# Head projections of a ViT tower in split format: resonances written twice, weights stacked

## The reference, cut to what matters

```python
def holo_linear(x, basis, phase, amp):
    resonance = jnp.einsum('bli,hi->blh', x, basis)      # 32 harmonics
    w = amp * jnp.cos(phase)
    return jnp.einsum('blh,oh->blo', resonance, w)
q = split_heads(holo_linear(x, basis_q, phase_q, amp_q))
k = split_heads(holo_linear(x, basis_k, phase_k, amp_k))
v = split_heads(holo_linear(x, basis_v, phase_v, amp_v))
attn = jax.nn.softmax(jnp.einsum('bhqd,bhkd->bhqk', q, k) * scale, axis=-1)
```

## Time and profile before

| what | us |
|---|---|
| median of 3 runs | 2207.89 (2204.55 to 2208.34) |
| the profiled execution | 2204.59 |
| its span in the trace | 2202.8 |
| outside the span | 1.8 |
| stage_a with its set-up, about | 0 to 1130 |
| one step of stage_a in the middle | 33.54 (key projections at 560.07 and 593.61) |
| PE busy, of the span | 2081.1 |

### The profile page before, as it was taken

How to read it: one execution, slowest core, us unless ns; L and a number is a source line. 1 busy time by engine, 2 the same in 40 slices (tenths; PEclk the granted TensorE clock), 3 DMA queues, 4 the chain that set the end, 5 groups by cost and what they waited for, 6 DMA issues and landing times. The chain is left out here.

```text
span 2202.8 us, 42583 instructions
## 1 busy us (share of the span) xinstructions
PE 2081.1 (94%) x15678; PEld 1847.7 (84%) x15678; DVE 1436.8 (65%) x3061; ACT 991.9 (45%) x2044; POOL 684.3 (31%) x737
## 2 busy tenths in 40 slices
PE   5899999999999999999889999999999999999998
PEld 4677777787887877777758999989998888889998
DVE  7677777777777877777644444677754444445666
ACT  2155555455555555554553333322225555554332
POOL 4334334233243343342202111000013333333665
PEclk9999999999999999999999999999999999999999
DMA  2533433424334233344214343000013333334665
GB/s 76 84 66 64 85 62 77 81 54 89 70 65 85 66 73 82 62 80 71 50 39 155 120 135 130 27 23 30 30 44 99 106 104 104 106 103 121 183 182 157
DMA packets 125274, 189.25 MB, mean 86 GB/s; under 512 B 23153, under 2 KB 76418, under 8 KB 125074
## 3 DMA queue, kind: packets, MB, share of 16 engines
q1 hardware_dynamic: 101232, 134.65, 26.0%
q0 software_dynamic: 12736, 34.69, 5.6%
q10 hardware_dynamic: 11106, 17.19, 2.4%
HBM read 84.32 MB, written 49.58 MB: 61 GB/s over the span
## 5 line engine op out<-in xcount | busy, mean ns | idle before, releaser
L675 ACT ACTIVATE pT<-ps 128x514 f32<-128x514 f32 x512 | 304.9, 597 | 308.7 <-PE ps L485 304.0
L842 DVE TENSOR_REDUCE mx<-ps 128x2 f32<-128x512 f32 x512 | 340.7, 680 | 106.1 <-PE ps L468 106.0
L2001 POOL DMA_INDIRECT z<-zd,itab x136 | 128.3, 944 | 470.2 <-DVE itab L1914 253.5
L468 PE MATMUL ps<-km,q 112*128 112x256 f32 x1024 | 246.0, 327 | 16.3 <-DMA km<-klo 10.5
L485 PE MATMUL ps<-q,km 114*128 114x258 f32 x1024 | 228.7, 305 | 31.5 <-ACT pT L675 31.5
L485 PEld LDWEIGHTS ps<-q,km 114*128 114x128 f32 x1024 | 159.1, 189 | 81.0 <-ACT pT L675 54.3
L1291 PE MATMUL ps<-zhi,whi 128*128 128x256 f32 x1056 | 218.4, 289 | 2.5 <-issue 2.4
L468 PEld LDWEIGHTS ps<-km,q 112*128 112x128 f32 x1024 | 166.7, 191 | 58.3 <-issue 24.9
L1291 PE MATMUL ps<-zhi,wlo 128*128 128x256 f32 x1056 | 214.7, 285 | 0.0
L1291 PE MATMUL ps<-zlo,whi 128*128 128x256 f32 x1056 | 213.9, 284 | 0.0
L1319 ACT ACTIVATE sil<-ps 128x512 f32<-128x512 f32 x132 | 79.0, 598 | 264.6 <-PE ps L1291 264.6
(11 more groups left out here) (320 smaller groups left out, 4997.5 us busy)
## 6 DMA issues: line engine op xcount, KB each, us to landing
yd<-raws SPq DMA_DIRECT2D x136, 128.0 KB, 1.8
q<-qhi SPq DMA_DIRECT2D x128, 129.0 KB, 4.1
km<-khi SPq DMA_DIRECT2D x256, 64.5 KB, 3.2
xs<-in_x SPq DMA_DIRECT2D x64, 256.0 KB, 4.4
z<-hscr SPq DMA_DIRECT2D x46, 256.0 KB, 2.9
raws<-in_wu SPq DMA_DIRECT2D x12, 768.0 KB, 4.8
hscr<-h SPq DMA_DIRECT2D x34, 256.0 KB, 5.1
zd<-z SPq DMA_DIRECT2D x33, 256.0 KB, 2.0
```

What stands on the lines that cost most here:

```text
L468: last = pe.matmul(ps[:, i % 2, k * L:(k + 1) * L], q2[p % U][0:MAXROW, QAT[g], t * P:(t + 1) * P], km[p % 2][0:MAXROW, k, g, 0:L], start= ...
L675: act.activation(pT[:, 2 * g:2 * g + 2, t, :], ps[:, score_bank(b, n):score_bank(b, n) + 2, 0:N], ACT.Exp, scale=HD ** -0.5).then_inc(s_ok, 1)
L842: dve.tensor_reduce(mx[:, t, 2 * QAT[g]:2 * QAT[g] + 2], ps[:, i % 2, :].rearrange("p (k l) -> p k l", k=2), AX_X, ALU.max, negate=True).t ...
L2001: pool.indirect_dma_start(zg(i), None, zd_rows, bass.IndirectOffsetOnAxis(itab[:, i:i + 1], 0)).then_inc(zg_in[i % NG], 16)
```

## The change

`resonances` has 128 output rows in place of 96: the basis of the queries is laid down a second time behind q, k and v. ACT writes all 128 rows rounded to `rhi` (float32r). Then ACT copies the rounded rows of the keys (rows 32 to 63 of `rhi`) to rows 96 to 127 of a second tile `rlo`, and DVE (`res_low`) writes the remainder, PSUM minus `rhi`, to rows 0 to 95 of `rlo`. A weight tile `wst` holds for q and k the rounded weight in its own 32 rows and the weight's remainder in rows 96 to 127, and for v the rounded weight and its remainder in two slots. A projection of q or k is then two float32r matmuls for each half of the channels (one over 96 rows, one over 128), one of v is three for each half of the positions. `Wz` moves to a temporary area and serves only the class token; the class token's resonances go to `rcls`. `res_low` stands in DVE's list at n = 3 behind `mixer_ekv`. `heads_qk(j, 0)` waits for both writes of ACT and for DVE's.

```diff
-    basT = sb("basT", [P, FT, 3 * HARM])
+    basT = sb("basT", [P, FT, P])
-    Wz = sb("Wz", [3 * HARM, 3, D])
+    wst = sb("wst", [P, 4, D], F32R)
-    rT = sb("rT", [3 * HARM, NP])
+    rcls = sb("rcls", [3 * HARM, NP - L])
+    rhi = sb("rhi", [P, L], F32R)
+    rlo = sb("rlo", [P, L], F32R)
+    Wz = temp(3, D)[0:3 * HARM]
...
-                last = pe.matmul(ps[0:3 * HARM, 6, 0:L], basT[:, f, :], zT[:, f, 0:L], ...)
+                last = pe.matmul(ps[:, 6, 0:L], basT[:, f, :], zT[:, f, 0:L], ...)
...
         def heads_qk(j, n):
             if n == 0:
-                pe.wait_ge(r_ok, j + 1)
+                if j == 0:
+                    pe.wait_ge(w_ok, 2)
+                pe.wait_ge(r_ok, 2 * j + 2)
+                pe.wait_ge(rl_ok, j + 1)
             else:
                 pe.wait_ge(lo_ok, 2 * j + 1)
+            whole, part = ((rhi, rlo), (rlo, rhi))[n]
             for f in range(FT):
-                last = pe.matmul(ps[:, 6, f * L:(f + 1) * L], Wz[:, n, f * P:(f + 1) * P], rT[:, 0:L], start=True, stop=True)
+                pe.matmul(..., wst[0:3 * HARM, n, f * P:(f + 1) * P], part[0:3 * HARM, :], start=True, stop=False)
+                last = pe.matmul(..., wst[:, n, f * P:(f + 1) * P], whole[:], start=False, stop=True)
...
         def heads_v(m):
-                last = pe.matmul(..., rT[:, t * P:(t + 1) * P], Wz[:, 2, :], start=True, stop=True)
+                mm = ((rhi, 2), (rlo, 2), (rhi, 3))
+                for i, (x, n) in enumerate(mm):
+                    last = pe.matmul(..., x[0:3 * HARM, t * P:(t + 1) * P], wst[0:3 * HARM, n, :], ...)
...
                     if n == 3:
                         act.wait_ge(r_ps, b + 3)
-                        act.activation(rT[:, 0:L], ps[0:3 * HARM, 6, 0:L], ACT.Copy).then_inc(r_ok, 1)
+                        if later(b + 2):
+                            act.wait_ge(v_ps, b + 2)
+                        act.activation(rhi[:], ps[:, 6, 0:L], ACT.Copy).then_inc(r_ok, 1)
+                        act.wait_ge(r_ok, 2 * b + 5)
+                        act.activation(rlo[3 * HARM:P, :], rhi[HARM:2 * HARM, :], ACT.Copy).then_inc(r_ok, 1)
...
+        def res_low(j):
+            dve.wait_ge(r_ok, 2 * j + 1)
+            dve.tensor_tensor(rlo[0:3 * HARM, :], ps[0:3 * HARM, 6, 0:L], rhi[0:3 * HARM, :], ALU.subtract).then_inc(rl_ok, 1)
...
                 if has(b + 3) and n in (2, 3):
                     mixer_ekv(b + 3, n - 2)
+                if has(b + 2) and n == 3:
+                    res_low(b + 2)
...
         dve.memset(Wz[:], 0.0)
+        dve.memset(wst[:].bitcast(F32), 0.0)
...
+        dve.wait_ge(w_ok, 1)
+        for n in range(2):
+            rows = slice(n * HARM, (n + 1) * HARM)
+            dve.tensor_copy(wst[rows, n, :], Wz[rows, n, :])
+        rows = slice(2 * HARM, 3 * HARM)
+        chain(dve.tensor_copy(wst[rows, 2, :], W[rows, :]))
+        for n in range(2):
+            rows = slice(n * HARM, (n + 1) * HARM)
+            dve.tensor_tensor(wst[3 * HARM:P, n, :], Wz[rows, n, :], wst[rows, n, :], ALU.subtract)
+        rows = slice(2 * HARM, 3 * HARM)
+        dve.tensor_tensor(wst[rows, 3, :], W[rows, :], wst[rows, 2, :], ALU.subtract).then_inc(w_ok, 1)
```

More of the change, by code:

```diff
@@ L175, in stage_a @@
     clso = sb("clso", [P, G, B])
-    (c_load, c_set, d_step, half_ok, mask_ok, wb_ok, ew_ok, arg_ok, cos_ok, w_ok, clsvar_ok, clsrs_ok, clsz_ok, clsT_ps,
-     clsT_ok, clsr_ps, clsr_ok, clsqkv_ps, spread_ok, mix_in) = (
+    (c_load, c_set, d_step, half_ok, mask_ok, wb_ok, ew_ok, arg_ok, cos_ok, w_ok, clsvar_ok, clsrs_ok, clsz_ok, cls_ps,
+     clsT_ok, clsr_ok, spread_ok, mix_in) = (
         sem(x) for x in ("c_load", "c_set", "d_step", "half_ok", "mask_ok", "wb_ok", "ew_ok", "arg_ok", "cos_ok", "w_ok",
-                         "clsvar_ok", "clsrs_ok", "clsz_ok", "clsT_ps", "clsT_ok", "clsr_ps", "clsr_ok", "clsqkv_ps",
+                         "clsvar_ok", "clsrs_ok", "clsz_ok", "cls_ps", "clsT_ok", "clsr_ok",
                          "spread_ok", "mix_in"))
@@ L191, in stage_a @@
     wo_in, vb_ok, vb_in, roh_ok = sem("wo_in"), sem("vb_ok"), sem("vb_in"), sem("roh_ok")
+    rl_ok = sem("rl_ok")
     r_ps, r_ok, qk_ps, v_ps, v_ok, hi_ok, lo_ok = (
@@ L420, in resonances @@
             for f in range(FT):
-                last = pe.matmul(ps[0:3 * HARM, 6, 0:L], basT[:, f, :], zT[:, f, 0:L], start=(f == 0), stop=(f == FT - 1))
+                last = pe.matmul(ps[:, 6, 0:L], basT[:, f, :], zT[:, f, 0:L], start=(f == 0), stop=(f == FT - 1))
             last.then_inc(r_ps, 1)
@@ L426, in heads_qk @@
             if n == 0:
-                pe.wait_ge(r_ok, j + 1)
+                if j == 0:
+                    pe.wait_ge(w_ok, 2)
+                pe.wait_ge(r_ok, 2 * j + 2)
+                pe.wait_ge(rl_ok, j + 1)
             else:
                 pe.wait_ge(lo_ok, 2 * j + 1)
+            whole, part = ((rhi, rlo), (rlo, rhi))[n]
             for f in range(FT):
-                last = pe.matmul(ps[:, 6, f * L:(f + 1) * L], Wz[:, n, f * P:(f + 1) * P], rT[:, 0:L], start=True, stop=True)
+                pe.matmul(ps[:, 6, f * L:(f + 1) * L], wst[0:3 * HARM, n, f * P:(f + 1) * P], part[0:3 * HARM, :], start=True, stop=False)
+                last = pe.matmul(ps[:, 6, f * L:(f + 1) * L], wst[:, n, f * P:(f + 1) * P], whole[:], start=False, stop=True)
             last.then_inc(qk_ps, 1)
@@ L437, in heads_v @@
             for t in range(LT):
-                last = pe.matmul(ps[:, 6, t * D:(t + 1) * D], rT[:, t * P:(t + 1) * P], Wz[:, 2, :], start=True, stop=True)
+                mm = ((rhi, 2), (rlo, 2), (rhi, 3))
+                for i, (x, n) in enumerate(mm):
+                    last = pe.matmul(ps[:, 6, t * D:(t + 1) * D], x[0:3 * HARM, t * P:(t + 1) * P], wst[0:3 * HARM, n, :],
+                                     start=(i == 0), stop=(i == len(mm) - 1))
             last.then_inc(v_ps, 1)
@@ L608, in _ @@
             last = pe.matmul(ps[:, 6, f:f + 1], clsz[:, f * P:(f + 1) * P], one1[:], start=True, stop=True)
-        last.then_inc(clsT_ps, 1)
+        last.then_inc(cls_ps, 1)
         pe.wait_ge(clsT_ok, 1)
         for f in range(FT):
-            last = pe.matmul(ps[0:3 * HARM, 5, 16:17], basT[:, f, :], zT[:, f, CLS:N], start=(f == 0), stop=(f == FT - 1))
-        last.then_inc(clsr_ps, 1)
+            last = pe.matmul(ps[0:3 * HARM, 5, 16:17], basT[:, f, 0:3 * HARM], zT[:, f, CLS:N], start=(f == 0), stop=(f == FT - 1))
+        last.then_inc(cls_ps, 1)
         pe.wait_ge(clsr_ok, 2)
@@ L617, in _ @@
             for f in range(FT):
-                pe.matmul(ps[:, 4, n * FT + f:n * FT + f + 1], Wz[:, n, f * P:(f + 1) * P], rT[:, CLS:N], start=True,
+                pe.matmul(ps[:, 4, n * FT + f:n * FT + f + 1], Wz[:, n, f * P:(f + 1) * P], rcls[:, 0:1], start=True,
                           stop=True)
         pe.matmul(ps[0:NH, 7, 0:D], rbc[:], Wz[:, 2, :], start=True,
-                  stop=True).then_inc(clsqkv_ps, 1)
+                  stop=True).then_inc(cls_ps, 1)
         filler(5, 12)
@@ L757, in _ @@
         act.activation(tr[:], tn[:], ACT.Sin).then_inc(cos_ok, 1)
-        act.wait_ge(clsT_ps, 1)
+        act.wait_ge(cls_ps, 1)
         act.activation(zT[:, :, CLS:N], ps[:, 6, 0:FT].rearrange("p (f o) -> p f o", o=1), ACT.Copy).then_inc(clsT_ok, 1)
-        act.wait_ge(clsr_ps, 1)
-        act.activation(rT[:, CLS:NP], ps[0:3 * HARM, 5, 16:17].broadcast_to([3 * HARM, 2]), ACT.Copy).then_inc(clsr_ok, 1)
+        act.wait_ge(cls_ps, 2)
+        act.activation(rcls[:], ps[0:3 * HARM, 5, 16:17].broadcast_to([3 * HARM, 2]), ACT.Copy).then_inc(clsr_ok, 1)
         mixer_norm(0, 0)
@@ L990, in _ @@
         dve.wait_ge(clsr_ok, 1)
-        dve.tensor_copy(rbc[:], rT[:, CLS:N].broadcast_to([3 * HARM, NH])).then_inc(clsr_ok, 1)
+        dve.tensor_copy(rbc[:], rcls[:, 0:1].broadcast_to([3 * HARM, NH])).then_inc(clsr_ok, 1)
         attn_stats(0, 0)
-        dve.wait_ge(clsqkv_ps, 1)
+        dve.wait_ge(cls_ps, 3)
         chain(dve.tensor_copy(clsh[:], ps[:, 4, 0:2 * FT].rearrange("p (n f) -> p n f", n=2)))
@@ L2067, in layout @@
     o["lnb"] = f(np.tile(t["tok_ln_b"][None], (P, LT)))
-    o["basT"] = tiles(np.concatenate([t["attn_basis_" + n].T for n in "qkv"], axis=1))
+    o["basT"] = tiles(np.concatenate([t["attn_basis_" + n].T for n in "qkvq"], axis=1))
     o["basoT"] = tiles(np.tile(t["attn_basis_o"].T, (1, 3)))
```

## The result

The changed kernel takes 2230.39 us in the median (4 runs, 2224.74 to 2232.83), the kernel before 2208.11 beside it (4 runs, 2204.55 to 2209.77). The ratio is 1.0097, with a 95% interval from 1.0077 to 1.0118: 17 to 26 us slower. The profiled execution took 2224.74 with a span of 2222.9, which is 20.1 us more than before.

A forecast was written before the change was run, and what follows sets the result against it. PE was busiest, but DVE set the stretch to L398. 30 steps x 0.61 = 18.3 plus 1.3 set-up made 19.6 us: 2224.2 from the profiled execution, 2227.5 from the median, forecast 2226, range 2217 to 2236.

The forecast's parts named there:

- The wait and its cause: Queries' projection: PE must wait for DVE's subtraction, which stands behind `ekv`, itself waiting for `ek`; 0.90 us.
- Its size: PE starts the queries' projection at 590.56 instead of 589.66, 0.90 us later, with 0.05 from DVE to PE.
- The projection behind the wait: Queries' projection after the wait: 0.22 + 3 x 0.12 = 0.58 us long, where it was 0.87.
- Per step: Each stage_a step gets 0.61 us longer, bounds 0.43 to 0.87, and nothing later gives it back.
- The keys' saving: Keys' projection, behind the first L390: 0.39 us less PE work, lost in a longer wait at L398, 0.76.
- The values' saving: Values' projection: 0.15 us less PE work, lost waiting for ACT's exponential; gain 0, at most 0.15.
- ACT's second write: ACT's copy of 32 x 256 before `ek`: about 0.4 us, in idle time, so it costs nothing even at 0.6.
- Set-up: Before the steps: 1.1 us for the memset of `wst` and 0.2 for six small operations, together 1.3.
- How many steps: The loss falls in 30 steps, b = -1 to 28; the first absorbs it, the last about breaks even.
- the savings count after all: Rival, no change: stretch to L398 and exponentials not binding, +0.07 us a step, 2209; chance 0.10.
- the subtraction is not late: Rival, faster: subtraction ready before PE wants the queries' projection, 2197, or 2179 with all savings; chance 0.08.
- The falling clock: Rival: PE, 92% busy in place of 95%, is granted a lower clock, costing tens of us; chance 0.03.

The follow-up runs named there:

- e1: The changed kernel with DVE's subtraction directly in front of `ekv` instead of behind it: 2209.47 us, 1.0012 of the kernel before.
- e5: The kernel before plus a DVE subtraction into a scratch tile behind `ekv`, which the unchanged queries' projection waits for: 2236.72 us, 1.0143 of the kernel before.
- e7: The changed kernel with one semaphore for ACT's writes and the subtraction, so the queries' projection waits once instead of twice: 2224.53 us, one run.
- e3: The changed kernel without the remainder passes of keys and values (two matmuls for four, two for six): 2230.00 us, 1.0100 of the kernel before.
- e2: The changed kernel with the subtraction in front of both maxima reductions of n = 3: 2216.08 us, 1.0054 of the kernel before.
- e8: The changed kernel without DVE's subtraction and the wait for it, rows 0 to 95 of `rlo` staying zero: 2199.59 us, one run.
- e11: A second run of the changed kernel with the subtraction in front of both maxima reductions, no filler: 2213.00 us, 1.0026 of the kernel before.
- e10: The changed kernel with the subtraction between the two maxima reductions, plus two useless matmuls at n = 8: 2194.37 us, 0.9948 of the kernel before.
- e6: The changed kernel with the subtraction in front of both maxima reductions, plus two useless matmuls in PE's `rden` wait: 2198.25 us, 0.9968 of the kernel before.
- e9: The kernel before plus two useless 512-column matmuls at n = 8, in front of PE's wait for `rden`: 2205.48 us, ratio 0.9999.

## Why the prediction was right, step by step

The forecast was 2226 and slower; 2230.39 was measured. In ratios, the forecast's sum of 19.6 us is 1.0089, inside the interval around 1.0097. The mechanism was right; that the sum fits the 20.1 us of the profiled executions so closely is in part luck, since a step taken too small (by 0.06, about 2 us in all) met a set-up taken too dear (by 0.65) and about one step too many.

- **The wait and its cause: right.** e1 and e5 show it from both sides: the order alone makes the loss, and the wait alone, put into the kernel before, makes 0.99 us a step.
- **Its size: 0.90 predicted, 1.00 found.** (The median of 28 steps is 0.98.) The chain was the predicted one (L383's end 564.02, `ek`, `ekv`, subtraction from 564.82 to 565.23), with a subtraction of 0.41 for 0.42. The term that was too small is the way from DVE to PE: 0.15, not 0.05. e7 shows that two waits in a row instead of one make that difference. The estimate of 0.39 for the subtraction from the Trainium skill ("VectorE: DVE Perf Modes", the section on the TRN2 errata) lies 0.02 below the 0.409 measured.
- **The projection behind the wait: 0.58 predicted, 0.55 found.** The first distance is 0.19, not 0.22, the later ones 0.12. The formula of the Trainium skill ("TensorE: Matmul & The Clock Gate", on the back-to-back issue gap), which that section gives for an isolated matmul and not for a stream with weight loads, makes an estimate of 0.109; the distances inside this projection are 0.116 and more.
- **Per step: 0.61 predicted, 0.67 found** (33.54 to 34.21).
- **The keys' saving gains nothing: right, the place of the loss wrong.** I had the whole 0.39 turn up as a longer wait at L398 (now L402), 0.76. It is 0.47, only 0.10 more than before. The missing part is lost before that, where `values` waits for DVE's residual: it starts 0.20 later behind the scores (0.44 in place of 0.24), and the next matmul follows it after 0.28 in place of 0.21. The same stretch of DVE rules both, so the sum did not change; from `rden` to L402 it is 6.66 us in both kernels (568.97 to 575.63; 560.02 to 566.68).
- **The values' saving gains nothing: right.** The scores behind that projection start 1.20 after those in front of it in both kernels (582.62 to 583.82 after, 572.08 to 573.28 before). e3 took out another 0.48 there, without effect.
- **ACT's second write costs nothing: right.** It takes 0.415 and `ek` still starts 0.04 behind L383's end.
- **Set-up: 1.3 predicted, about 0.65 found** (the first `zT` at 50.11 in place of 49.46). The memset of `wst` takes the 0.91 + 0.16 predicted, but the cast behind it, which had lasted 2.44 from 10.67, now lasts 1.37 from 11.74: both end at 13.11. The memset was covered. The six small operations, 2.2 us with 1.7 of cover, cost 0.5 in place of the 0.2 predicted; the first `rden` was already 0.26 late in front of them (30.72 in place of 30.46).
- **How many steps: 30 predicted.** The first gives no difference (32.39 and 32.36 to the next), the second only 0.10, the third 0.56, the rest 0.67. That sums to about 19.4 in quiet steps, as much as 29 full ones; the measured distance from the first to the last `zT` grew by 21.1 us, and I put the rest down to steps with late transfers or the lower clock. Behind the last `zT` the changed kernel is 1.7 us shorter (1110.8 and 1112.5); it has 20 us at the lower clock there, the kernel before 24.

Of the rivals, "the savings count after all" is refuted by e3, "the subtraction is not late" by the profile. The falling clock was no part of this result (one fall), yet it decided e2.

What stays open: the fall's rule. The changed kernel has the same two waits (0.45 and 0.47) and even less busy PE (897 us from 100 to 1080, against 919 in e2 and 924 before), and it had one fall there while e2 and e8 had five and e11 eight. The kernels with the pair of waits and a quiet step of 33.50 or more have one or two falls, those with a shorter step five to eight; these are single profiled executions, and I know no reason for it. In e11 most of the falls lie about 68 us apart, two of its steps. And e2's extra time at the lower clock lies more behind stage_a than in it: 31 of its 75 us stand between 1180 and 1340, where the kernel before has 10 and the instructions are the same. I have no experiment that explains either. That fewer falls came with the filler is measured, in the time as in the clock; why is not.

## What to carry to other kernels

A consumer that needs one more operation waits for whatever stands in front of that operation in its engine's list. Here the subtraction took 0.41 us, and its place behind an instruction with a wait of its own cost 1.0 us a step; moved up in front of the second reduction it is free (e10's quiet step is e8's). Of two places that both look early enough, e2's still cost 0.16, because it pushed back a reduction that PE waits for.

Before counting a saving on the busiest engine, find for each place the wait that ends next behind it. Of 0.93 us a step only 0.38 was ever gained (e8, e10).

When a step gets shorter and the kernel does not, look at the granted clock of each run before looking for a stall. A filler in a covered wait of PE is then worth a try, with the same filler in the kernel before as control.

## What the runs showed of the hardware

- Two semaphore waits in a row in front of a matmul delayed it by 0.09 us against a single wait (0.15 and 0.06 behind the releaser's end, in every step compared), although the other semaphore had been counted about 2 us before (ACT's second write ends at 563.15, PE starts at 565.38).
- PE's clock went to the lower level (PEclk 0.50 to 0.56 over 3 us) directly behind two waits of about 0.45 us that were 0.5 us apart: all 23 falls in the middle of stage_a stand there, in seven kernels. Most such pairs had no fall behind them. With the second wait at 0.37 (two kernels) or with two matmuls of 512 columns in it (e6, e9, e10) there was none.
- The kernel's time follows the clock of its run closely: for the kernel before, 2199.07 at a mean clock of 0.996 and 2213.39 at 0.986. Differences below 0.3% between two kernels need that column beside them.
